# Spectral stage: the product with W2 in three passes of split operands

## The reference, cut to what matters

```python
_, U = jnp.linalg.eigh(L_norm)
agg = jnp.einsum('mn,bnd->bmd', U.T, features)
h = jax.nn.relu(agg @ W1 + b1)          # 256 -> 128 features
out = h @ W2 + b2                       # 128 -> 256 features
x = layernorm(x + jnp.einsum('nm,bmd->bnd', U, out))
```

## Time and profile before

| | |
|---|---|
| median of 3 runs | 2170.86 us (2170.53 to 2171.2) |
| the profiled execution, its own time | 2171.96 us |
| its span, first to last instruction | 2170.2 us |
| mean granted TensorE clock | 0.939 |
| PE busy over the span | 1808.6 us (83%) |
| DVE busy | 1457.8 us (67%) |
| ACT busy | 868.0 us (40%) |
| POOL busy | 653.2 us (30%) |

### The profile page before, as it was taken

How to read it: one execution, slowest core, us unless ns; L and a number is a source line. 1 busy time by engine, 2 the same in 40 slices (tenths; PEclk the granted TensorE clock), 3 DMA queues, 4 the chain that set the end, 5 groups by cost and what they waited for, 6 DMA issues and landing times. The chain is left out here.

```text
span 2170.2 us, 31902 instructions
## 1 busy us (share of the span) xinstructions
PE 1808.6 (83%) x9508; PEld 1524.7 (70%) x9508; DVE 1457.8 (67%) x5806; ACT 868.0 (40%) x1784; POOL 653.2 (30%) x1040
## 2 busy tenths in 40 slices
PE   3454333326999999999999999999999998979997
PEld 2333333314988888888899999888887886857774
DVE  7999999985778555445444444444444777858886
ACT  2333222201344466333333333232332656646664
POOL 0001344402233466333323332413341113521111
PEclk9999766656999999999999999999999999989999
DMA  6000000000111000000000000000010412200111
GB/s 189 2 2 1 1 1 1 1 1 20 59 49 40 20 19 15 10 10 10 5 11 10 10 10 0 20 1 0 0 39 20 165 59 71 97 30 30 40 40 49
DMA packets 44689, 62.70 MB, mean 29 GB/s; under 512 B 13969, under 2 KB 33297, under 8 KB 44433
## 3 DMA queue, kind: packets, MB, share of 16 engines
q1 hardware_dynamic: 43968, 61.08, 8.3%
q10 hardware_dynamic: 592, 0.17, 0.0%
HBM read 36.08 MB, written 25.17 MB: 28 GB/s over the span
## 5 line engine op out<-in xcount | busy, mean ns | idle before, releaser
L2272 ACT ACTIVATE l_gates<-ps,biases 128x512 f32<-128x512 f32 (+1 forms) x504 | 288.9, 635 | 490.6 <-remote 476.2
L2143 PE MATMUL ps<-l_nodes_in,l_even 128*128 128x512 f32 x1392 | 321.4, 391 | 2.6 <-DVE x L1562 1.9
L2143 PEld LDWEIGHTS ps<-l_nodes_in,l_even 128*128 128x128 f32 x1392 | 260.9, 188 | 59.0 <-DVE x L1562 2.7
L2143 PE MATMUL ps<-l_nodes_in,kept 128*128 128x336 f32 (+1 forms) x1280 | 298.0, 350 | 1.9 <-ACT l_gates L2272 1.8
L2369 DVE TENSOR_TENSOR l_gates<-l_gates 128x512 f32<-128x512 f32 (+1 forms) x72 | 50.2, 697 | 343.3 <-ACT l_gates L2272 343.3
L2059 POOL CAST l_nodes_in<-big 128x512 fp32r (+3 forms) x142 | 100.3, 735 | 548.1 <-remote 520.0
L2143 PEld LDWEIGHTS ps<-l_nodes_in,kept 128*128 128x128 f32 x1280 | 229.4, 188 | 27.3 <-issue 4.3
L2143 PE MATMUL ps<-l_state,l_even 128*128 128x512 f32 x960 | 223.3, 392 | 0.0
L2143 PEld LDWEIGHTS ps<-l_state,l_even 128*128 128x128 f32 x960 | 180.4, 188 | 39.7
L2062 POOL TENSOR_TENSOR l_nodes_in<-big,l_nodes_in 128x512 fp32r<-128x512 f32 (+1 forms) x142 | 200.5, 1433 | 5.7
L995 PE MATMUL ps<-w,sw_xT 128*128 128x128 f32 x256 | 60.5, 431 | 129.6 <-ACT sw_xT L859 129.6
(11 more groups left out here) (561 smaller groups left out, 3909.7 us busy)
## 6 DMA issues: line engine op xcount, KB each, us to landing
x<-in_x SPq DMA_DIRECT2D x4, 2048.0 KB, 16.8
residual<-s_x SPq DMA_DIRECT2D x16, 512.0 KB, 2.6
x<-residual SPq DMA_DIRECT2D x16, 512.0 KB, 7.8
normed<-l_raw SPq DMA_DIRECT2D x16, 512.0 KB, 2.6
x<-normed SPq DMA_DIRECT2D x16, 512.0 KB, 3.2
out<-a_y SPq DMA_DIRECT2D x16, 512.0 KB, 2.8
l_raw<-in_L_gnn_W SPq DMA_DIRECT2D x16, 256.0 KB, 2.8
l_raw<-in_L_gnn_W SPq DMA_DIRECT2D x4, 512.0 KB, 3.6
```

Source lines behind the costliest of these rows:

```text
L2143: return pe.matmul(ps[:, 4 * j + gate, 0:n], weight[w_part][:, at:at + 128].bitcast(F32R), src[:, part, k, 0:n].bitcast(F32R), start=start ...
L2272: act.activation(gates[:, j, gate, 0:n], ps[:, 4 * j + gate, 0:n], ACT.Tanh if gate == G else ACT.Sigmoid, bias=bias[:, gate * KD + j:gate ...
```

## The change

W2 is split once into a high and a low part (tile `w2`), by two VectorE instructions ahead of the first step. ScalarE writes the mixed features as `float32r` into the high half of `mixed`; a new VectorE instruction a group, `low_mixed`, subtracts this from bank MIXED and writes the low half. `out0` becomes 8 matmuls with the high half, a wait on the low half, and 4 matmuls with it. `mix_hidden(g)` and the last `convolve2`, which write bank MIXED again, now wait for `low_mixed` and not for `move_mixed`. `low_mixed(s)` stands on VectorE between the low parts of `agg2` and of `agg1`.

```diff
-    hid, mixed = sb("hid", [128, GROUP]), sb("mixed", [128, GROUP])
+    hid, mixed = sb("hid", [128, GROUP]), sb("mixed", [128, 2, GROUP])
+    w2 = sb("w2", [128, 2, WIDTH])
...
         def mix_hidden(g):
             pe.wait_ge(hid_ready, g + 1)
             if g:
-                pe.wait_ge(uh_moved, g)
+                pe.wait_ge(mixed_low, g)
...
         def out0(g):
             pe.wait_ge(uh_moved, g + 1)
             if g:
                 pe.wait_ge(ln.added, g)
+            else:
+                pe.wait_ge(w2_split, 2)
             for i in range(TILES):
-                mm = pe.matmul(Z[:, i, :], mixed[:, i * TILE:(i + 1) * TILE], w["w2"][:, :], start=True, stop=True)
+                for w_part in PARTS:
+                    pe.matmul(Z[:, i, :], mixed[:, HIGH, i * TILE:(i + 1) * TILE].bitcast(F32R),
+                              w2[:, w_part, :].bitcast(F32R), start=w_part == HIGH and i % 2 == 0, stop=False)
+            pe.wait_ge(mixed_low, g + 1)
+            for i in range(TILES):
+                mm = pe.matmul(Z[:, i, :], mixed[:, LOW, i * TILE:(i + 1) * TILE].bitcast(F32R),
+                               w2[:, HIGH, :].bitcast(F32R), start=False, stop=i % 2 == 1)
             mm.then_inc(z_ready, 1)
...
             else:
-                pe.wait_ge(uh_moved, GROUPS)
+                pe.wait_ge(mixed_low, GROUPS)
...
-            act.activation(mixed[:, :], MIXED, ACT.Copy).then_inc(uh_moved, 1)
+            act.activation(mixed[:, HIGH].bitcast(F32R), MIXED, ACT.Copy).then_inc(uh_moved, 1)
...
+        dve.tensor_copy(w2[:, HIGH].bitcast(F32R), w["w2"][:, :]).then_inc(w2_split, 1)
+        dve.wait_ge(w2_split, 1)
+        dve.tensor_tensor(w2[:, LOW].bitcast(F32R), w["w2"][:, :], w2[:, HIGH], ALU.subtract).then_inc(w2_split, 1)
+
+        def low_mixed(g):
+            dve.wait_ge(uh_moved, g + 1)
+            dve.tensor_tensor(mixed[:, LOW].bitcast(F32R), MIXED, mixed[:, HIGH], ALU.subtract).then_inc(mixed_low, 1)
...
                 low(s - 3, b_moved, agg2, B, b_low)
+            if s < GROUPS:
+                low_mixed(s)
             if 2 <= s < GROUPS + 2:
                 low(s - 2, a1_moved, agg1, A1, a1_low)
```

More of the change, by code:

```diff
@@ L1618, in spectral_and_mixing @@
     (u_ready, u_summed, hid_ready, uh_ready, uh_moved, z_ready, x_shifted, a1_ready, a1_moved, g_ready, g_summed,
-     h1_ready, b_ready, b_moved, a1_low, b_low, c_ready, c_summed, big_written, x1_stored, shift_ready, raw_landed, split) = (
+     h1_ready, b_ready, b_moved, a1_low, b_low, c_ready, c_summed, big_written, x1_stored, shift_ready, raw_landed, split, mixed_low, w2_split) = (
         sem(s) for s in (
@@ L1622, in spectral_and_mixing @@
             "a1_moved", "g_ready", "g_summed", "h1_ready", "b_ready", "b_moved", "a1_low", "b_low", "c_ready", "c_summed",
-            "big_written", "x1_stored", "shift_ready", "raw_landed", "split"))
+            "big_written", "x1_stored", "shift_ready", "raw_landed", "split", "mixed_low", "w2_split"))
     A1 = ps[:, 0:2, :]
```

## The result

The changed kernel takes 2167.78 us (median of 22 runs, 2166.79 to 2169.91); the kernel before, on the same chip, 2171.42 us (22 runs, 2170.28 to 2174.45). The ratio is 0.9983, 95% interval 0.9976 to 0.9990: 3.6 us or 0.17% faster. The profiled execution has a span of 2165.9 us.

The account below looks back on a forecast made before the run. TensorE's own list sets the pace from step 3 to 15: 14 x 0.29 = 4.06 us, less 0.5 at the start, gives 3.6 us off the 2170.86 median, so 2167.3 us; own range 2166.3 to 2168.9, with rivals 2165.8 to 2170.0.

Parts of the forecast that it names:

- The rival by columns alone: `out0`: new matmuls one 0.108 us pass each, gain 0.43 us a group; 2165.4 us, or 2166.5 capped; chance 0.09.
- the one in which weight loads set the distance: `out0`: weight loads not hidden, twelve matmuls take 2.28 us, a loss of 8.2 us, time 2179; chance 0.05.
- The margins of 0.56, 0.06 and 0.03 us: Steady-step slack: VectorE's gap after `low_mixed` 0.56, A1's copy ahead of `convolve1` 0.06, VectorE ahead of `bias1` 0.03 us.
- a wait takes the place of the gain: Steady step: `low_mixed` or A1's copy becomes the bound, half or more of the gain lost, 2170 us; chance 0.13.
- the 0.82 that I had as the most: Stage start: two W2 instructions take up to 2 x 0.41 = 0.82 us in VectorE's 3.80 us idle time, cost 0.
- a toll of 0.5 us: Stage start: first statistics wait for `low_mixed(1)`, 0.65 us later, of which 0.5 us was taken as lasting.
- the case in which the second rise comes at the same moment: Step 2: clock rise stays in place, so half of the 0.65 us delay comes back, 0.33 left.
- two cases in step 2: Step 2: clock rise at the same moment leaves 0.33 of 0.65 us; if it moves with the work, all stays.
- one moment, 515.3, in step 1: Stage start: clock rises only at about 515.3, so part of `mix_hidden(1)` runs slowly; copy earlier by 0.2 to 0.55 us.

Follow-up runs that it names:

- e4: Changed kernel with a fourth pass, low x low, so 16 float32r matmuls a group in `out0`: 2176.59 us, ratio 1.0019 to the kernel before.
- e2: Changed kernel without the subtraction `low_mixed` and its waits; the last four matmuls read the high half: 2167.46 us, ratio 0.9977 to the kernel before.
- e1: Changed kernel without the pass high features x low part of W2, 8 matmuls a group and not 12: 2167.71 us, ratio 0.9981 to the kernel before.
- e5: Changed kernel with `low_mixed(1)` moved behind the first statistics on VectorE: 2167.28 us, ratio 0.9971 to the kernel before.
- e9: Kernel before with three unread plain matmuls in step 2 and two ahead of `convolve2(15)`: 2169.78 us, ratio 0.9984.
- e6: Changed kernel with four unread plain matmuls in step 2 ahead of `mix_hidden(2)`: 2167.32 us, ratio 0.9975 to the kernel before.
- e7: Changed kernel with `low_mixed(1)` behind the first statistics and unread matmuls, two in step 2, two ahead of `convolve2(15)`: 2165.58 us, ratio 0.9962 to the kernel before.

## Why the prediction was right

*The matmul distances.* Predicted 0.120 us from `convolve1`'s rows, measured 0.119, and 0.48 us for a pass of four (e4). The step: 12.37 predicted, 12.38 measured. From the second aggregation to the LSTM the stage is 192.36 - 188.65 = 3.71 us shorter, 0.285 for each of 13 steps. The rival by columns alone is out, and so is the one in which weight loads set the distance: a LDWEIGHTS of L1665 or L1669 takes 0.19 us on average and stays hidden. One reading was loose: the stationary operand isn't changed for each of `convolve1`'s matmuls; in the high part two in a row have the same one. It is loaded for each all the same, and the distance is 0.119 to 0.120 us either way.

The Trainium skill, "TensorE: Matmul & The Clock Gate", section "Back-to-back issue gap", has N/2.4 + 2.5 ns for an isolated matmul at the fast clock, by which an estimate for 256 columns is 109 ns. This trace doesn't agree for `float32r` (0.119 us). A record of a plain float32 matmul takes 0.216 us, which is what the formula gives if the record counts as 512 columns.

*The margins of 0.56, 0.06 and 0.03 us.* The subtraction fitted into the gap with 0.66 left and cost nothing (e2). The copy of A1 was 0.06 us from becoming the bound: e1 took the step to 12.32, where the sum from the rows had it. VectorE ahead of `bias1` has no gap left, and no cost shows. The rival "a wait takes the place of the gain" is out for this change, and right for the next one (e1).

*The start.* The two instructions on W2 took 0.29 and 0.58 us, together a little over the 0.82 that I had as the most, and cost nothing: the first `bias0` starts 2.09 us after the stage's first matmul, with and without them. Then I took a toll of 0.5 us, less the gain of `out0(2)`, so +0.2 at the second aggregation. Two traces with the rise at the same place (before 11.0, the change's second trace 11.1) give 31.40 - 31.46 = -0.06. On the way the first statistics are 0.47 late (0.45 to 0.8 was forecast) and `mix_hidden(2)` 0.46 late (19.07 against 18.61 us). With the 0.29 of `out0(2)` taken out, 0.23 of it is left at the second aggregation, half of the 0.46: that is the case in which the second rise comes at the same moment (24.7 us in both), which I had given with 0.33, and not the 0.5 that I took. The matmuls at the slow level were 0.235 us apart ((514.35 - 512.47)/8, in that second trace), where I took 0.24:

```profile
512.47 2.07 PE L1665 MATMUL ps<-s_w,s_mixed 128*128 128x256 f32 x8 [0.69 <-ACT s_mixed L1751]
...
514.35 1.05 PE L1669 MATMUL ps<-s_w,s_mixed 128*128 128x256 f32 x4
...
518.03 1.39 DVE L1568 BATCH_NORM_STATS2 s_lnstats<-s_lnr 128x6 f32<-128x256 f32 x4
```

So the mechanism was right to about a quarter of a us, for two traces with like clocks; I had read the clock's first rise as fixed. That was the weak spot: I gave it two cases in step 2 and one moment, 515.3, in step 1, from a single trace. It was seen from 6.9 to 15.5 us after the stage's start, and an early one turns the toll of 0.47 into a lead of 0.66 (12.38 - 11.72).

*The total.* Forecast 3.6 us, measured 3.6 in 22 against 22 runs. Agreement to a tenth is luck: the interval is 2.2 to 5.2 us. I wrote that runs lie within 0.7 us; that was read from three, and the 22 of the kernel before lie within 4.2. The two traces with like clocks have the LSTM's first matmul 3.77 us apart (223.81 and 220.04 after the first matmul). That the gain isn't given back in the LSTM is seen at its start (4.61 us earlier in the first pair of traces, 728.09 to 723.48) and in the span (4.3 us); the 0.3 us between them I haven't followed up. The second pair has 3.5 us at both places (728.72 to 725.22, 2171.0 to 2167.5).

## What to carry to other kernels

When one engine is full for a whole stretch, take the distance between starts of an instruction of exactly the new form from the same trace; it gave the step to 0.01 us. Three passes on split operands beat a plain float32 matmul here by 17% (1.44 against 1.73 us), and a fourth loses it. Before shortening the bound engine's work, list what would be late next and by how much: a margin of 0.06 us meant that a third less work (e1) brought 0.06 us a step. In the first steps of a pipeline, a new instruction that waits on a later group can be dear even if it is free in the steady state: the place of one line was worth 1.3 us at the first statistics (e5), though the total was too noisy to show it. And where the bound engine idles and its clock falls behind it, matmuls that nobody reads can be worth as much as the change itself: 2.9 us on the kernel before, with three of them in step 2 and two at the end (e9).

## What the runs showed of the hardware

- The clock's rise at the start of the stage came between 6.9 and 15.5 us after the first matmul, and differed by 4 us between two executions of the changed kernel, whose second aggregations are 1.0 us apart. In the two of before the first rise differs by 0.4 us and the second one differs by 3 us; their second aggregations are 1.5 us apart. So a single trace per kernel can't be used for a difference of that size at such a place.
- In the ten traces without fillers in step 2 the clock fell to the 1.2 GHz level there, behind or in PE's idle time; in the three with them (e6, e7, e9) it stayed at 1.00.
- Idle time of TensorE of 2.46 us ahead of the stage's last product was followed by a slow spell (a granted clock of 0.55 to 0.60 over the next microseconds) in two of ten traces (before's second, e5), where the product took 4.57 and 4.30 us; in the others it took 2.97 to 3.00.
- A `float32r` matmul with a LDWEIGHTS of its own starts 0.119 us after the one before for 256 columns at the 2.4 GHz level, 0.235 us at the 1.2 GHz level. One record of a plain float32 matmul, two of which make one product, takes 0.216 us for the same columns.
- Where a `float32r` matmul follows a plain one, the trace shows its start too early: in the changed kernel the first record of L1665 starts 0.030 us after the last of `aggregate1`, whose own are 0.112 apart, and the second one 0.201 us behind it, where the rest are at 0.119. The two distances make 0.231 us, as 0.112 and 0.119 do. So only whole steps were compared, not the lines at such a border.
